# Six windows of gathered rows instead of four, and a new order of gathers, roots and scatters on GpSimd

## What is computed

```python
xn = layernorm(x)                                   # over 512 channels, eps 1e-5
msg = relu(xn[src] + edge_attr @ W_e + b_e)         # 5000 x 512, edge_attr is 5000 x 64
aggr = segment_sum(msg, dst, num_segments=10000)
h = (1 + eps) * xn + aggr
h = silu(batchnorm(h @ W1 + b1))                    # 512 -> 1024
h = silu(batchnorm(h @ W2 + b2))                    # 1024 -> 512
x = x + h
x = x + mixture_ffn(layernorm(x))                   # 16 experts, top token per group
```

## Time and profile before

| | |
|---|---|
| median of 3 executions | 1988.45 us (1987.42 to 1990.15) |
| profiled execution, its time | 1996.32 us |
| profiled execution, its span | 1994.6 us |
| PE busy | 93% of the span |
| DVE, ACT, POOL busy | 60%, 49%, 18% |
| first scatter starts | 73.40 us |
| first load after the last scatter | 208.10 us |
| granted TensorE clock, mean | 0.973 |

### The profile page before, as it was taken

The page is one execution under the profiler, slowest core; times in us unless marked ns, Lnnn a source line. Parts: engine busy times, 40 slices in busy tenths (PEclk is TensorE's granted clock), DMA queues, the critical chain, the costliest instruction groups (busy, mean ns, idle before and its releaser), DMA issues. The chain is left out here.

```text
span 1994.6 us, 41286 instructions
## 1 busy us (share of the span) xinstructions
PE 1851.7 (93%) x15896; PEld 1361.5 (68%) x15896; DVE 1189.4 (60%) x2345; ACT 986.9 (49%) x1716; POOL 363.8 (18%) x428
## 2 busy tenths in 40 slices
PE   5486799999999999999999968999999999999999
PEld 3354678888888878888888766666666566666654
DVE  6488466666666543333333266776767767667655
ACT  2355223333333275665665345665656656556553
POOL 4486220000000000000000042222222222222210
PEclk9778899999999999999999999999999999999999
DMA  9987755666665373433443164444444435344322
GB/s 368 300 158 102 184 145 173 186 180 181 178 171 164 113 280 126 166 140 123 143 165 123 68 202 132 148 126 129 142 131 123 153 109 151 122 131 140 107 66 80
DMA packets 162434, 305.68 MB, mean 153 GB/s; under 512 B 15505, under 2 KB 87185, under 8 KB 159090
## 3 DMA queue, kind: packets, MB, share of 16 engines
q1 hardware_dynamic: 153327, 282.66, 44.8%
q0 software_dynamic: 8960, 20.98, 5.5%
HBM read 168.72 MB, written 134.87 MB: 152 GB/s over the span
## 5 line engine op out<-in xcount | busy, mean ns | idle before, releaser
L1542 PE MATMUL bank<-f2s,inner_bd 128*32 128x512 f32 x2528 | 295.5, 596 | 1.1 <-issue 1.0
L1425 ACT ACTIVATE inter_hi<-bank 128x512 fp32r<-128x512 f32 x316 | 188.3, 600 | 206.3 <-PE bank L1542 205.0
L598 ACT ACTIVATE h1o<-bank,b_by_channel 128x500 f32<-128x500 f32 x160 | 108.5, 678 | 324.8 <-PE bank L430 316.3
L1347 DVE TENSOR_TENSOR inter_lo<-bank,inter_hi 128x512 fp32r<-128x512 f32 x316 | 215.8, 689 | 88.2 <-ACT inter_hi L1425 87.2
L428 PE MATMUL bank<-hhi,w_hi 128*128 128x500 f32 x624 | 244.7, 392 | 0.0
L430 PE MATMUL bank<-hhi,w_lo 128*128 128x500 f32 x624 | 243.6, 390 | 0.0
L429 PE MATMUL bank<-hlo,w_hi 128*128 128x500 f32 x624 | 242.6, 389 | 0.0
L428 PE MATMUL bank<-ahi,w_hi 128*128 128x500 f32 x608 | 237.3, 390 | 0.0
L429 PE MATMUL bank<-alo,w_hi 128*128 128x500 f32 x608 | 236.6, 389 | 0.0
L430 PE MATMUL bank<-ahi,w_lo 128*128 128x500 f32 x608 | 236.4, 389 | 0.0
L562 DVE BATCH_NORM_STATS2 stats<-h1o 128x500 f32 (+1 forms) x160 | 103.3, 676 | 155.7 <-ACT h1o L598 155.7
(11 more groups left out here) (149 smaller groups left out, 3354.4 us busy)
## 6 DMA issues: line engine op xcount, KB each, us to landing
h1T<-h1o SPq DMA_DIRECT2D x19, 2000.0 KB, 8.1
h1in<-h1T SPq DMA_DIRECT2D x19, 2000.0 KB, 9.7
aggregate<-at SPq DMA_DIRECT2D x20, 1024.0 KB
x<-in_x SPq DMA_DIRECT2D x79, 256.0 KB, 2.7
x<-x SPq DMA_DIRECT2D x79, 256.0 KB, 3.4
x_back<-x SPq DMA_DIRECT2D x79, 256.0 KB, 3.1
out<-x_back SPq DMA_DIRECT2D x79, 256.0 KB, 2.1
h2in<-h2T SPq DMA_DIRECT2D x39, 512.0 KB, 4.1
```

What stands on the lines that cost most here:

```text
L598: nc.scalar.activation(h1o[b][:, m, :], mb[m % 4][:, 0:CW], ACT.Identity, bias=b1c[:, m:m + 1]).then_inc(evr, 1)
L1347: nc.vector.tensor_tensor(ilo[b][:, :], bI[b][:, :], ihi[b][:, :].bitcast(F32), ALU.subtract).then_inc(ilr, 1)
L1425: nc.scalar.activation(ihi[b][:, :], bI[b][:, :], ACT.Copy).then_inc(ihr, 1)
L1542: last = nc.tensor.matmul(bI[b][32 * i:32 * i + 32, :], ibd[:, e, j, :, :].rearrange("p s g -> p (s g)"), f2s[:, e, :], start=True, stop=True)
```

## The change

The number of window buffers goes from four to six. The tile `xg` keeps its size; windows 4 and 5 are put into the buffers of the first chunk of x and of its normalized copy. So SyncE waits, before it loads that chunk, for the last `mlr` of window 4. GpSimd's order becomes: 24 gathers (windows 0 to 5), roots of windows 0 to 4, wait for the zeros, and then for each w: scatter(w), three gathers (tiles 24+3w to 26+3w; in round 5 only tile 39, from round 6 none), and from round 1 on the root of window w+4. The other edits are names: `rows_of(t)` in place of `xg[:, slot(t), :]`.

```diff
-XW = 4
+XW = 6
+GW = 3
...
-        xg = sb("xg", [P, XW * EW, H])
+        xg = sb("xg", [P, (XW - 2) * EW, H])
+        groups = [xg[:, w * EW:(w + 1) * EW, :] for w in range(XW - 2)] + [first["xt"][0], first["ht"]]
...
-        def slot(t):
-            return t % (XW * EW)
+        def rows_of(t):
+            return groups[t // EW % XW][:, t % EW, :]
...
                 rows = x[0:CW, :].rearrange("(j p) h -> p j h", p=RT)
+                sp.wait_ge(mlr, EW * (XW - 1))
                 for p0, p1 in ((0, RT // 16 * 16), (RT // 16 * 16, RT)):
...
-                def gather(w):
+                def gather(t):
+                    w = t // EW
                     if w >= XW:
 
                         pool.wait_ge(mhr, EW * (w - XW + 1))
                         pool.wait_ge(mlr, EW * (w - XW + 1))
-                    for t in window(w):
-                        nc.gpsimd.indirect_dma_start(
-                            out=xg[:, slot(t), :], out_offset=None, in_=x, in_offset=bass.IndirectOffsetOnAxis(
-                                ap=scol[:, t:t + 1], axis=0)).then_inc(gat[w % XW], 16)
+                    nc.gpsimd.indirect_dma_start(
+                        out=rows_of(t), out_offset=None, in_=x, in_offset=bass.IndirectOffsetOnAxis(
+                            ap=scol[:, t:t + 1], axis=0)).then_inc(gat[w % XW], 16)
...
                 pool.wait_ge(lds, 16)
-                for w in range(XW):
-                    gather(w)
+                for t in range(XW * EW):
+                    gather(t)
                 for w in range(XW - 1):
                     root(w)
                 for i in range(ZQ):
                     pool.wait_ge(zeroed[i], 16 * len(pieces[i::ZQ]))
                 for w in range(EN):
                     scatter(w)
-                    if w + XW < EN:
-                        gather(w + XW)
-                    if w + XW - 1 < EN:
-                        root(w + XW - 1)
+                    for t in range(XW * EW + GW * w, min(XW * EW + GW * (w + 1), ET)):
+                        gather(t)
+                    if w >= 1 and w + XW - 2 < EN:
+                        root(w + XW - 2)
```

More of the change, by code:

```diff
@@ L155, in messages @@
                     for t in window(w):
-                        s = slot(t)
                         act.wait_ge(prr, t + 1)
-                        nc.scalar.activation(xg[0:EP, s, :], xg[0:EP, s, :], ACT.Relu, bias=nb[0:EP, t:t + 1]).then_inc(msr, 1)
+                        nc.scalar.activation(rows_of(t)[0:EP, :], rows_of(t)[0:EP, :], ACT.Relu, bias=nb[0:EP, t:t + 1]).then_inc(msr, 1)
                         act.wait_ge(msr, t + 1)
@@ L161, in messages @@
                             act.wait_ge(cpr, EW * (w - 1))
-                        nc.scalar.activation(mhi[0:EP, t % (2 * EW), :], xg[0:EP, s, :], ACT.Copy).then_inc(mhr, 1)
+                        nc.scalar.activation(mhi[0:EP, t % (2 * EW), :], rows_of(t)[0:EP, :], ACT.Copy).then_inc(mhr, 1)
                 def collect(w):
@@ L281, in statistics @@
                     for t in window(w):
-                        nc.vector.bn_stats(st[0:EP, t, :], xg[0:EP, slot(t), :]).then_inc(bst, 1)
+                        nc.vector.bn_stats(st[0:EP, t, :], rows_of(t)[0:EP, :]).then_inc(bst, 1)
                     for t in window(w):
@@ L297, in combine @@
                         dve.wait_ge(emr, t + 1)
-                        nc.vector.scalar_tensor_tensor(out=xg[0:EP, slot(t), :], in0=xg[0:EP, slot(t), :],
+                        nc.vector.scalar_tensor_tensor(out=rows_of(t)[0:EP, :], in0=rows_of(t)[0:EP, :],
                                                        scalar=rs[0:EP, t:t + 1], in1=emb[t % EW][0:EP, :],
@@ L304, in combine @@
                         dve.wait_ge(mhr, t + 1)
-                        nc.vector.tensor_tensor(mlo[0:EP, t % (2 * EW), :], xg[0:EP, slot(t), :],
+                        nc.vector.tensor_tensor(mlo[0:EP, t % (2 * EW), :], rows_of(t)[0:EP, :],
                                                 mhi[0:EP, t % (2 * EW), :].bitcast(F32), ALU.subtract).then_inc(mlr, 1)
```

## The result

The changed kernel takes 1997.18 us, the median of 6 executions (1995.11 to 1999.42), against 1989.39 us for 6 of the kernel before (1987.42 to 1992.5). The ratio is 1.0037, 95% interval 1.0027 to 1.0047: slower by 7.8 us by the medians, 5 to 9 by the interval. The forecast was +9.8 us, 1998.3.

What follows compares the result with a forecast made beforehand. GpSimd's scatters and the compute loop, nearly equal in speed, were taken to bound the edge stage; its end 78.3 + 90.2 + 49.4 = 217.9 for 208.1, +9.8 us, gave 1998.3, range 1991.5 to 2004.5.

Steps and rivals of the forecast that it cites:

- Step 1: Zeroing before the first scatter: eight more gathers displace zeros on full DMA engines, first scatter 73.4 to 78.3, +4.9 us.
- Rival 3: Roots don't hold scatters and zeros aren't lengthened: first scatter stays at 73.4, -5.9 us, 1982.5; chance 0.07.
- rival 4: Outstanding gathers hold GpSimd during zeroing: first scatter up to 84.5, +16 us, about 2004; chance 0.09.
- Step 2: First scatter to sums of window 3: these start 26.0 us after it instead of 31.3, 5.3 us earlier.
- Step 3: Scatters of windows 2 to 5: each waits for root(w+4), so rounds go at the compute loop's 14.2 us.
- second term: First scatter to scatter(6): 90.2 us for 85.3, +4.9; about 1.5 from steps 2 and 3, 3.4 from the stall.
- Step 4: Tile 39's gather, behind scatter(5), lands late: VectorE stalls 3.4 us before window 9's statistics, delaying root(9) and scatter(6).
- rival 1: Tile 39 lands within 1.2 us of its issue's end, so VectorE doesn't wait: +6.4 us, 1994.9; chance 0.13.
- Step 5: From scatter(6) to the stage's end rounds go by landing of scatters, as before: 49.4 us.
- bound of -2.0: Lower bound on the second term from the compute loop's pace, 13.7 to 14.3 us a window over four windows.
- The signs: Expected timeline marks: scatters 2 to 5 14.2 us apart, GpSimd idle 2 to 3 us before roots 6 to 9.
- rival 2: Roots don't hold scatters: scatter(2) at Z (first scatter's start) + 29.0, end 207.1, -1.0 us, 1987.5; chance 0.12.

Runs made afterwards that it cites:

- the gathers alone: Kernel before plus eight gathers nobody reads, issued during zeroing, the load of x's first chunk waiting for them; ratio 1.0015 to the kernel before.
- roots as before: Changed kernel with only its roots put back: windows 0 to 2 ahead of the zeros' wait, then root(w+3) in round w; ratio 0.9983 to the kernel before.
- second profile: The changed kernel run once more, unaltered; ratio 1.0043 to the kernel before, edge stage ended at 212.88 us.
- gathers in fours: Changed kernel with roots put back and the 16 late gathers in fours (rounds 0 to 3) instead of threes; ratio 0.9992 to the kernel before.
- both edits: Changed kernel with roots put back and tile 39 gathered in round 4; ratio 0.9989 to the kernel before, stage ended at 203.31 us.

## Why the prediction was right

**Step 1, the zeros (+4.9).** Right: 78.52 for 78.3, and 4.76 us with the gathers alone. Root(4) ended at 77.6 for 77.2, 0.9 us ahead of the scatter, and without it, with the roots as before, the first scatter came at 78.32: the zeros held it. Rival 3 is out with that, and rival 4 too: all 24 gathers went out in 0.94 to 1.23 us each until 36.24.

**Step 2, to the sums of window 3.** VectorE's subtractions ended 103.61 - 78.52 = 25.1 us after the first scatter, for 25.6; before it was 104.35 - 73.40 = 31.0. The compute loop did get ahead by 5.9 us (5.3 forecast), as the change promises.

**Step 3, the roots.** The mechanism is right, and shown by putting them back. Scatter(2) came at 78.52 + 29.3, for 30.0. Its share in the second term, 1.5 us, was too large: without the stall, scatter(6) came 0.4 us later after the first scatter than before in one profile (88.75 - 85.26 - 3.09) and 1.8 us earlier in the other.

**Step 4, tile 39 (3.4 us).** 3.09 and 2.79 us. VectorE went on 3.5 and 3.2 us after the end of its issue, not 4.45 to 4.86, so rival 1 had a part of it: here one gather behind scatters came sooner than four, but not within the 1.2 us at which nobody would wait.

**Step 5, the tail.** 216.11 - 167.27 = 48.8 for 49.4.

**What was mis-sized** is above all the pace of the compute loop within steps 3 and 4: I took 14.2 us a window from before, and the changed kernel had 56.3 / 4 = 14.1 (159.90 - 103.61) in one profile and rounds of 13.7 in the other. From the first scatter to scatter(6) it was 88.75 and 86.25 us, for 90.2: too high by 0.7 and 1.4 at scatter(2), by 0.4 and 2.0 in the four rounds behind it, and by 0.3 and 0.6 in the stall. In the first profile this and the shorter tail (0.6) make the stage end at 216.1 for 217.9, and the ratios, +7.4 and +8.6 us, agree with that. In the second profile the stage ended at 212.9, 5 us below the sum; of that the bound of -2.0 covered the pace. How close the forecast of the stage came is known only to these 3 us.

**The signs.** The scatters of windows 2 to 5 came 14.2 us apart on average in the first profile and 13.7 in the second. GpSimd was to idle 2 to 3 us before roots 6 to 9; it idled 2.12, 0.80, 0.79 and 6.51. The prediction's own figures, 12.7 us of work in rounds of 14.2, gave 1.5 and not 2 to 3. The measured 0.8 in the rounds of 13.8 says that GpSimd's work there took 13.0.

**What I had wrong** stands in rival 2. I called the moved load of x one that costs nothing, and took Z + 29.0 for scatter(2) without roots from the kernel before. But those 29.0 contained both the load beside scatter(1) and a fourth gather. With four gathers and the load late it was 101.17 - 73.38 = 27.8 in the kernel before and 106.40 - 78.71 = 27.7 with gathers in fours; with three gathers it was 104.66 - 78.32 = 26.3. So of the 2.7 us the load had about 1.2 and the gather about 1.4. The tail had another 1.3 (48.1 for 49.4), and the end was 203.4, not 207.1. In the changed kernel the roots hid the first two. So rival 2, had it come, would have been 3.4 us faster by the ratio, and not the 1.0 that I gave it.

## What to carry to other kernels

A deeper buffer moves a due time; look at every small instruction that is moved along with it. Here a root of 1 us, put one window further ahead, tied the scatters to statistics that come two windows later, and cost 10.7 us by the ratios. Without it the rest, the buffers, the spacing and the later load together, was worth about 8 (10.7 + 4.8 for the zeros - 7.4 for the whole), an estimate from ratios that are good to 2 us or so. Work put into an idle queue isn't free if the DMA engines are full: price it in bytes. And when a chain goes by landings, see which bulk loads start beside it, and where a moved load will stand instead: here the late load of x took 1.3 us off one round and put 2.1 on another, and the late load of W1 and the vectors took off 1.2 and put on 3.0.

## What the runs showed of the hardware

- With the DMA share at 1.01, 2.10 MB more of gathers moved the end of the zeros by 4.77 us (72.57 to 77.34), 440 GB/s, and 24 gathers went out without being held, though the second four had landed only at 28.8, when 18 had been issued.
- A load of 1 MB that started 3.0 and 4.0 us after the first of four accumulating scatters lengthened the round by 1.3 to 2.1 us (15.1 for 13.8, 16.1 for 14.0). Started 0.2 us after the first, it left the round at 12.5 and 12.6 (roots as before, and both edits).
- Four scatters took 11.2 to 12.8 us from the first issue to the start of what waits for their landing in the last four rounds of all profiles, but 13.18 and 13.12 in two rounds of the run in fours. Why is open.
- The part of the program behind the stage, the same in all kernels, took 1777 to 1782 us in eleven profiles and 1786.5 in one.
